# A conditioned transformer and Mamba kernel: loads in the order of use, and where the modulations are computed

## What is computed

```python
# layer 0, as one sequence sees it (t = 256, c = 256, 16 heads of 16)
mod = silu(condition) @ Wada + bada                   # 6 x 256
sh_a, sc_a, gt_a, sh_m, sc_m, gt_m = split(mod)
xm = layernorm(x, g1, be1) * (1 + sc_a) + sh_a
x = x + gt_a * (softmax(causal(q @ k.T / 4)) @ v @ Wproj + bproj)   # q, k, v = xm @ Wqkv
xm = layernorm(x, g2, be2) * (1 + sc_m) + sh_m
x = x + gt_m * (gelu(xm @ W1 + b1) @ W2 + b2)
# layer 1: (shift, scale, gate) = c @ adaln_w + adaln_b, twice
h = norm(x) * (1 + scale) + shift
x = x + gate * (ssm(h, fwd) + flip(ssm(flip(h), bwd)))
# ssm: xs, z = h @ in_w; dt, B, C = xs @ xproj_w; a scan over 256 steps,
# 512 channels x 64 states, with A = -exp(A_log); then (y + D * xs) * silu(z) @ out_w
x = x + gate * ((silu(h @ w1) * (h @ w2)) @ w3)
```

## Time and profile before

| what | value |
|---|---|
| median of 3 runs | 3541.03 us (3540.88 to 3542.23) |
| the profiled execution, its own time | 3532.22 us |
| its span in the trace | 3530.3 us |
| busy: PE, DVE, ACT, POOL | 87%, 81%, 87%, 83% |
| first projection starts | 55.99 us |
| prologue ends, first scan starts | 228.45 us |

### The profile page before, as it was taken

One profiled execution on the slowest core, in us unless ns is written; L12 is line 12 of the kernel. 1 busy time (PEld: TensorE's weight loads), 2 busy tenths in 40 slices (PEclk: granted clock), 3 DMA queues, 4 the chain that ended last, 5 costly groups with the idle time before them and its releaser, 6 DMA issues.

```text
span 3530.3 us, 70435 instructions
## 1 busy us (share of the span) xinstructions
PE 3064.4 (87%) x21944; PEld 2666.9 (76%) x21944; DVE 2872.2 (81%) x3122; ACT 3086.7 (87%) x6820; POOL 2941.0 (83%) x1551
## 2 busy tenths in 40 slices
PE   6878898898988999888998889889898899988776
PEld 4567787787877877787787778778777788877765
DVE  1249998799888998789888898889988898889885
ACT  1269999999899998899998999999998999999995
POOL 0049988899888998889888898889988899899995
PEclk9589999999999999999999999999999999999999
DMA  5011111111111111111111111111111111111211
GB/s 167 0 30 45 46 42 40 48 50 45 39 48 40 52 43 40 47 47 46 43 41 46 47 46 40 48 40 51 45 41 46 45 46 44 42 43 43 54 47 27
DMA packets 170750, 162.54 MB, mean 46 GB/s; under 512 B 25834, under 2 KB 165098, under 8 KB 170356
## 3 DMA queue, kind: packets, MB, share of 16 engines
q1 hardware_dynamic: 170356, 157.69, 16.3%
HBM read 154.44 MB, written 3.18 MB: 45 GB/s over the span
## 4 chain that ended last, share of the span: by engine, by line
PE 31%; POOL 23%; issue 20%; ACT 16%; DVE 7%; SPq 1%; POOLq 0%; DMA 0%; ACTq 0%; DVEq 0%
POOL hst L395 18%; PE ps L1175 8%; PE ps L1191 7%; ACT dA L574 7%; POOL uBT L404 6%; PE ps L944 5%; ACT uBT L560 4%; DVE hst L864 3%; PE ps L953 2%; PE ps L1013 2%; PE ps L1064 1%; PE ps L991 1%; PE ps L1000 1%; PE ps L1074 1%; SPq L301 1%
## 5 line engine op out<-in xcount | busy, mean ns | idle before, releaser
L395 POOL TENSOR_TENSOR hst<-hst,C_sb 128x1024 f32<-128x1024 f32 x1024 | 2427.1, 2385 | 324.4 <-DVE hst L864 317.5
L864 DVE TENSOR_TENSOR_SCAN hst<-dA,ps 128x512 f32<-128x512 f32 x2048 | 2383.8, 1203 | 258.7 <-ACT dA L574 135.8
L574 ACT ACTIVATE dA<-dt,A 128x255 f32<-128x255 f32 x4096 | 1779.6, 500 | 102.1 <-DVE hst L864 96.8
L1175 PE MATMUL ps<-ident,uBT 128*128 128x128 f32 x8192 | 1275.3, 280 | 153.8 <-DVE hst L864 116.5
L1191 PE MATMUL ps<-ident,hst 128*128 128x128 f32 x8192 | 1273.2, 279 | 141.8 <-POOL hst L395 139.3
L1175 PEld LDWEIGHTS ps<-ident,uBT 128*128 128x128 f32 x8192 | 993.1, 145 | 286.3 <-DVE hst L864 151.0
L1191 PEld LDWEIGHTS ps<-ident,hst 128*128 128x128 f32 x8192 | 971.2, 143 | 204.0 <-POOL hst L395 203.1
L560 ACT ACTIVATE uBT<-uT,BT 128x512 f32<-128x512 f32 x1536 | 1045.6, 714 | 32.6 <-PE ps L1175 31.6
L404 POOL TENSOR_TENSOR uBT<-uT,BT 128x512 f32<-128x512 f32 x512 | 551.7, 1078 | 227.0 <-ACT uT L517 220.1
L475 ACT ACTIVATE probs<-ps,nmax 128x128 f32<-128x128 f32 (+1 forms) x256 | 104.8, 418 | 73.6 <-DVE nmax L735 73.6
L1013 PE MATMUL ps<-qk 32*128 32x256 f32 (+1 forms) x512 | 163.0, 400 | 0.6 <-DVE v L711 0.6
(11 more groups left out here) (141 smaller groups left out, 2138.3 us busy)
## 6 DMA issues: line engine op xcount, KB each, us to landing
C_sb<-c_dram SPq DMA_DIRECT2D x1024, 128.0 KB, 2.9
gate_l<-gate_rows_dram SPq DMA_DIRECT2D x16, 256.0 KB, 3.9
x_att<-in_x_dram SPq DMA_DIRECT2D x8, 256.0 KB, 3.6
w<-in_L_cond_W_dram SPq DMA_DIRECT2D x2, 1024.0 KB
out_dram<-x_glu SPq DMA_DIRECT2D x8, 256.0 KB, 3.2
hst<-in_L_cond_Wada_dram SPq DMA_DIRECT2D x1, 1536.0 KB
wg<-in_L_cond_mlp_w_dram SPq DMA_DIRECT2D x3, 512.0 KB
w_xp<-_L_cond_fwd_xproj_w_dram SPq DMA_DIRECT2D x1, 1280.0 KB
```

Source lines behind the costliest of these rows:

```text
L395: pool.tensor_tensor(h, h, C_sb[:, n % FED:n % FED + 1, :].to_broadcast([P, KI, NB]), ALU.mult).then_inc(hC_ready.sem, 1)
L574: done = act.activation(dA[:, n % NT, c, lo:hi], dt[:, d, c, lo:hi], ACT.Exp, scale=A[:, d, c, n:n + 1])
L864: dve.tensor_tensor_scan(pair(hst[:, n % NR]), pair(dA[:, n % NT]), ps[:, BANK_U + (2 * n + e) % (2 * NT), :][:, way], 0.0, ALU.mult, ALU. ...
L1175: last = pe.transpose(ps[:, BANK_U + (2 * n + e) % (2 * NT), o:o + P], uBT[:, n % NF, j, c * P:(c + 1) * P], ident[:, :])
```

## The change

The loads are issued in another order, under six semaphores in place of two: `att_in` (columns, and of Wada the columns of the first norm, its shift and scale), then x, `qkv_in`, `mods_in` (gate biases, the rest of Wada, the adaln weights), `mlp_in`, `ssm_in` and `late_in`. Wqkv's queries and keys come as they are into the tile of `xsT` (`qk_raw`); DVE copies the query weights and POOL the key weights into the padded tiles. The weights of the second adaln move from the tile `qk`, which the projections now write early, to `uT`. PE computes two modulations (the shift and scale of the first norm) ahead of the first norm; the others, 12 by-channel pieces and the four rows, are pieces of a generator of which it takes one after each step of the first heads stage. DVE makes the first norm's scale and shift behind that norm's statistics (`setup_attention`), and everything else at the last step of the first heads stage (`setup_rest`). ACT computes exp(A) and the negation behind `layer0(0)`. The waits are set where each thing is used first.

```diff
@@ -231,7 +231,8 @@
-        wada1 = [flat(uBT[:, :, :, :].rearrange("p r k n -> p r (k n)"), 3 * D), flat(qk[:, :, :], 3 * D)]
+        wada1 = [flat(uBT[:, :, :, :].rearrange("p r k n -> p r (k n)"), 3 * D), flat(uT[:, :, :], 3 * D)]
+        qk_raw = flat(xsT[:, :, :], 2 * D)
         mod_rows = gT[0:B, :, :].rearrange("p a b -> p (a b)")
...
@@ -283,24 +286,28 @@
-            sp.dma_start(col_in[:, :], columns).then_inc(mods_in, 16)
+            def load(w, src, arrived):
+                sp.dma_start(w, src.rearrange("(k p) n -> p k n", p=P)).then_inc(arrived, 16)
+            sp.dma_start(col_in[:, :], columns).then_inc(att_in, 16)
+            load(wada[:, :, 0:2 * D], Wada[:, 0:2 * D], att_in)
+            sp.dma_start(x_att[:, :, :], x_tiles[:, 0:TT, :]).then_inc(x_in.sem, 16)
+            load(qk_raw, Wqkv[:, 0:2 * D], qkv_in)
+            load(wv[:, :, :], Wqkv[:, 2 * D:3 * D], qkv_in)
             sp.dma_start(gate_bias, rows[:, 0:4 * D].rearrange("a (i n) -> a i n", n=D)).then_inc(mods_in, 16)
-            sp.dma_start(wada, Wada.rearrange("(k p) n -> p k n", p=P)).then_inc(mods_in, 16)
-            sp.dma_start(wada1[0], wmamba.rearrange("(k p) n -> p k n", p=P)).then_inc(mods_in, 16)
-            sp.dma_start(wada1[1], wglu.rearrange("(k p) n -> p k n", p=P)).then_inc(mods_in, 16)
-            sp.dma_start(x_att[:, :, :], x_tiles[:, 0:TT, :]).then_inc(x_in.sem, 16)
-            sp.wait_ge(pads_zero, 2)
-            for w, c in ((wq, 0), (wk, 1)):
-                for k in range(KD):
-                    sp.dma_start(w[:, k, :, 0:HD], Wqkv[k * P:(k + 1) * P, c * D:(c + 1) * D]
-                                 .rearrange("p (h e) -> p h e", e=HD)).then_inc(weights_in, 16)
-            sp.dma_start(wv[:, :, :], Wqkv[:, 2 * D:3 * D].rearrange("(k p) n -> p k n", p=P)).then_inc(weights_in, 16)
-            loads = [(wproj, Wproj), (w1, W1), (w2, W2), (w_in[0], f_in), (w_in[1], b_in), (w_xp[0], f_xproj),
-                     (w_xp[1], b_xproj), (w_out[0], f_out), (w_out[1], b_out), (wg1, glu_w1), (wg2, glu_w2), (wg3, glu_w3)]
-            for w, src in loads:
-                sp.dma_start(w[:, :, :], src.rearrange("(k p) n -> p k n", p=P)).then_inc(weights_in, 16)
-            sp.dma_start(A[:, :, :, :].rearrange("p d k n -> p (d k n)"), A_log).then_inc(weights_in, 16)
-            sp.dma_start(bias_rows, rows[:, 4 * D:6 * D].rearrange("a (i n) -> a i n", n=D)).then_inc(weights_in, 16)
+            load(wada[:, :, 2 * D:6 * D], Wada[:, 2 * D:6 * D], mods_in)
+            load(wada1[0], wmamba, mods_in)
+            load(wada1[1], wglu, mods_in)
+            sp.dma_start(bias_rows, rows[:, 4 * D:6 * D].rearrange("a (i n) -> a i n", n=D)).then_inc(mlp_in, 16)
+            load(wproj[:, :, :], Wproj, mlp_in)
+            load(w1[:, :, :], W1, mlp_in)
+            load(w2[:, :, :], W2, mlp_in)
+            load(w_in[0][:, :, :], f_in, ssm_in)
+            load(w_xp[0][:, :, :], f_xproj, ssm_in)
+            sp.dma_start(A[:, :, :, :].rearrange("p d k n -> p (d k n)"), A_log).then_inc(ssm_in, 16)
+            for w, src in ((w_out[0], f_out), (w_in[1], b_in), (w_xp[1], b_xproj), (w_out[1], b_out),
+                           (wg1, glu_w1), (wg2, glu_w2), (wg3, glu_w3)):
+                load(w[:, :, :], src, late_in)
...
@@ -362,7 +369,11 @@
             sp.wait_ge(out_done.sem, out_done.at(NBLK - 1, 16))
 
-        N_MODS, N_WEIGHTS = 16 * 5, 16 * (5 + 12 + 2)
+        N_ATT, N_QKV, N_MODS, N_MLP, N_SSM, N_LATE = 16 * 2, 16 * 2, 16 * 4, 16 * 4, 16 * 3, 16 * 7
+        heads_at = STEPS["norm"] + STEPS["qkv"]
+        proj_at = heads_at + 2 * STEPS["heads"]
...
+            pool.wait_ge(pads_zero, 2)
+            pool.wait_ge(qkv_in, N_QKV)
+            pool.tensor_copy(wk[:, :, :, 0:HD], heads_of(1)).then_inc(wqk_ready, 1)
...
 
         @block.scalar
         def _(act):
-            act.wait_ge(mods_in, N_MODS)
+            act.wait_ge(att_in, N_ATT)
             act.activation(silu_col[:, :, :], cond_col, ACT.Silu).then_inc(silu_ready, 1)
             act.preload_act_table_set(LN_EXP)
-            act.wait_ge(weights_in, N_WEIGHTS)
-            act.activation(A[:, :, :, :], A[:, :, :, :], ACT.Exp).then_inc(A_ready, 1)
-            act.wait_ge(A_ready, 2)
-            act.wait_ge(mods_ready, 1)
             act.wait_ge(consts_ready, 7)
 
...
 
-            for _ in layer0(0):
-                pass
+            for i, _ in enumerate(layer0(0)):
+                if i == 4:
+                    act.wait_ge(att_mods, 1)
+                if i == proj_at - 1:
+                    act.wait_ge(mods_ready, 1)
+            act.wait_ge(ssm_in, N_SSM)
+            act.activation(A[:, :, :, :], A[:, :, :, :], ACT.Exp).then_inc(A_ready, 1)
+            act.wait_ge(A_ready, 1)
+            act.activation(A[:, :, :, :], A[:, :, :, :], ACT.Copy, scale=-1.0).then_inc(A_ready, 1)
+            act.wait_ge(A_ready, 2)
...
@@ -645,30 +663,47 @@
-            dve.wait_ge(mods_mm, 1)
-            dve.wait_ge(mods_in, N_MODS)
-            dve.tensor_copy(mod_rows, ps[0:B, 1:3, :].rearrange("p a n -> p (a n)")).then_inc(rows_ready, 1)
-            first(dve.tensor_tensor(mods[:, :, :, :].rearrange("p i k b -> p (i k) b"),
-                                    ps[:, 0, 0:16 * B].rearrange("p (i b) -> p i b", b=B),
-                                    mod_bias.rearrange("p i k -> p (i k)").unsqueeze(2).to_broadcast([P, 16, B]), ALU.add))
-
-            for s in range(4):
+            def modulations(lo, hi):
...
+            def scales(s):
...
-                    first(dve.tensor_tensor(mod_shift[:, s], mod_shift[:, s], mods[:, 2 * s], ALU.add))
-                else:
-                    first(dve.tensor_scalar(mod_scale[:, s], mods[:, 2 * s + 1], 1.0, None, ALU.add))
-                    first(dve.tensor_copy(mod_shift[:, s], mods[:, 2 * s]))
-            dve.wait_ge(A_ready, 1)
-            dve.tensor_scalar(A[:, :, :, :], A[:, :, :, :], -1.0, None, ALU.mult).then_inc(A_ready, 1)
-            dve.wait_ge(consts_ready, 7)
-            dve.wait_ge(weights_in, N_WEIGHTS)
-            for d in range(2):
-                for c in range(KI):
-                    dve.tensor_scalar(skip_diag[:, d, c, :], ident[:, :], D_col[:, d, c:c + 1], None, ALU.mult).then_inc(mods_ready, 1)
+                    return dve.tensor_tensor(mod_shift[:, s], mod_shift[:, s], mods[:, 2 * s], ALU.add)
+                first(dve.tensor_scalar(mod_scale[:, s], mods[:, 2 * s + 1], 1.0, None, ALU.add))
+                return dve.tensor_copy(mod_shift[:, s], mods[:, 2 * s])
+            def setup_attention():
+                dve.wait_ge(att_in, N_ATT)
+                dve.wait_ge(att_mm, 1)
+                modulations(0, 2)
+                scales(LN_ATT).then_inc(att_mods, 1)
+                dve.wait_ge(pads_zero, 2)
+                dve.wait_ge(qkv_in, N_QKV)
+                dve.tensor_copy(wq[:, :, :, 0:HD], heads_of(0)).then_inc(wqk_ready, 1)
+            def setup_rest():
+                dve.wait_ge(mods_mm, 1)
+                dve.tensor_copy(mod_rows, ps[0:B, 1:3, :].rearrange("p a n -> p (a n)")).then_inc(rows_ready, 1)
+                modulations(2, 8)
+                first(scales(LN_MLP))
+                first(scales(LN_SSM))
+                scales(LN_GLU).then_inc(mods_ready, 1)
+                dve.wait_ge(consts_ready, 7)
+                for d in range(2):
+                    for c in range(KI):
+                        dve.tensor_scalar(skip_diag[:, d, c, :], ident[:, :], D_col[:, d, c:c + 1], None, ALU.mult).then_inc(skip_ready, 1)
...
-            for _ in layer0(0):
-                pass
+            for i, _ in enumerate(layer0(0)):
+                if i == 0:
+                    setup_attention()
+                if i == heads_at + STEPS["heads"] - 1:
+                    setup_rest()
...
-            pe.wait_ge(silu_ready, 1)
-            pe.wait_ge(mods_in, N_MODS)
-            pe.wait_ge(consts_ready, 7)
             of_kind = [(wada, 1, 0), (wada, 1, 1), (wada, 1, 3), (wada, 1, 4),
                        (wada1[0], 0, 0), (wada1[0], 0, 1), (wada1[1], 0, 0), (wada1[1], 0, 1)]
             conds = (cond_col, silu_col)
-            for i, (w, cn, col) in enumerate(of_kind):
+            def modulation(i, m):
+                w, cn, col = of_kind[i]
+                o = (i * KD + m) * B
+                for k in range(KD):
+                    last = pe.matmul(ps[:, 0, o:o + B], w[:, k, col * D + m * P:col * D + (m + 1) * P], conds[cn][:, k, :],
+                                     start=(k == 0), stop=(k == KD - 1))
+                return last
+            def other_modulations():
+                pe.wait_ge(mods_in, N_MODS)
+                for i in range(2, 8):
+                    for m in range(KD):
+                        modulation(i, m)
+                        yield
+                for i, (w, cn, col) in enumerate(((wada, 1, 2), (wada, 1, 5), (wada1[0], 0, 2), (wada1[1], 0, 2))):
```

(42 more changed lines are left out.)

10 lines of the change are left out of this document (9 added, 1 removed).

## The result

The changed kernel took 3514.22 us, the median of 4 runs (3508.43 to 3518.37), against 3540.95 for the kernel before: 26.7 us less, a ratio of 0.9921 with an interval from 0.9905 to 0.9937. The forecast was 3515.6, 25.4 us less, in a range from 3500 to 3526. In a later series on one chip the same two kernels took 3518.3 (6 runs) and 3539.2 us (18 runs), 21 us apart. Executions in the slow state (in all three, of 3732, 8432 and 15633 us) are left out of every median here.

A forecast was written before the change was run, and what follows sets the result against it. Prologue loading was taken as the bound the change could move, each microsecond there counting at the end. 43.8 - 15.8 - 2.6 = 25.4 us less, so 3541.03 - 25.4 = 3515.6 us, range 3500 to 3526.

The forecast's parts named there:

- part 1: Prologue: reordered loads let the first norm and projections start early, first projection at 12.2 us, 43.8 us earlier.
- part 2: First heads stage: 36 modulation matmuls on PE, only partly covered by its idle time, add 15.8 us.
- part 3: Between the two heads stages: DVE's setup delays the ninth group's maximum by 2.6 us, at most 4.5.
- part 4: ACT's exp(A) and negation behind the prologue's last norm, and later load waits: 0 us; ACT's operations 1.3 us without cover.
- part 5: PE's clock rise at projections, MLP and SSM varies, 1.5 to 1.7 us each; taken as 0.
- the carry-over: Whole kernel: the runs' median lies 8.8 us above the profiled execution, assumed to hold after the change too.
- (a): Heads: filled heads keep PE's clock up, so modulations add about 0; 41.2 us gained, 3499.8 us; chance 0.12.
- (b): Nothing covers the additions: PE 21.3 us, DVE 4.5, copies or fetch 1, clock 3.4; 3527.4 us; chance 0.12.
- (c): Prologue: loads land out of issue order, x at worst at 39 us; 3548 to 3555 us, slower; chance 0.04.
- (d): Prologue: PE's queue reaches a wait early and holds the first projections, a few microseconds of 43.8; no separate chance.

The follow-up runs named there:

- The doubled set: Changed kernel with each of the 36 modulation matmuls among the heads issued twice; 3529.59 us (7 runs).
- the block: Changed kernel with the 36 other modulation matmuls in one block between the projections and the first heads stage; 3512.75 us (4 runs).

## Why the prediction was right

**Earlier start (part 1).** Right, 44.2 for 43.8. In order of issue and by bytes: silu at 5.10 (forecast 5.5), x at 5.8 (6.4), the raw weights at 8.2 (8.0), all at 41 (39). The copies were priced at no more than 1.08 us and took 0.62 and 0.42; with 1.6 us to spare they cost nothing.

**Modulations among heads (part 2).** Right, 15.1 for 15.8. The doubled set cost 20.3 for 21.2 us of matmuls, the block 17.8 over heads alone, and single ones in the gaps nothing: that PE is the bound in heads and offers half a microsecond a group is shown from three sides. The clock fell 3.7 us into heads, at 27.8 us, where about 4 us was put.

**DVE between the stages (part 3).** Right, 2.3 for 2.6; taking the diagonals out gave 1.56 of their 1.65 us back.

**Edits at nothing (part 4).** Right for the later waits: the stretch from the maximum to the first residual is the same to 0.1 us. Wrong for ACT's work on A, a term put at nothing that cost 1.3 us. The prediction set the two operations against the 8.25 us of idle time ahead of the silu, and these two are covered. It missed the table load that stands between the norm and that idle time in the kernel before, and that now runs behind the wait. Its price without cover, 1.3 us, was for the two operations and agrees by chance. No run puts exp(A) elsewhere, so that it is this move that holds the load back is read from the traces and not tested. In all, then, the change is worth 44.2 - 15.1 - 2.3 - 1.3 = 25.4 us, the very number of the forecast, because errors of 0.4, 0.7 and 0.3 us in the three terms happened to make up for the missed one.

**The clock (part 5) and the carry-over.** Here a term was mis-sized. I took 0 with a worst case of 3.4 us; between the two profiled executions it was 10.0 us ahead of the scan. The step behind it was that only the rise at the start of a dense stretch could vary, at the projections, the MLP and the SSM. The later rises came to 2.3 us, inside the worst case. The rows after show a second way, worth 7.8 us: a fall at the end of PE's 2.5 us wait for the gelu, which runs half of a product at half speed (3.3 us), and one in its 3.2 us wait for the silu, which slows the next three products (4.4). And the sum was made on an execution in which neither had happened: "3506.8 would be its counterpart" was wrong for the profiled one, 3518.4, and the first scan came at 213.1 us and not near 203. The median came out because carrying the 8.8 us over put such losses back in. The second profile of the kernel before, 3541.8 us, has 5.3 us of them ahead of the scan, in the MLP, and 4.3 behind it. That part was luck in the choice of row, not insight. The fall in the wait for the silu wasn't seen in the kernel before. Of the nine profiled executions with the longer wait it came in two, both of the changed kernel as it is, so whether it belongs to the change or to chance isn't shown.

**The rivals.** (a) That the filled heads hold the clock failed for the modulations and held for another filling: these two kinds of matmul didn't keep it up even with PE busy without a gap, while with two 256-column products with a full weight in each group it stayed up through all eight groups of the first stage. The Trainium skill's "TensorE: Matmul & The Clock Gate", section "What's actually happening", puts the clock down to how busy PE has been; the block of modulations, busy 18 of 18 us while the clock fell, disagrees if busy time is meant. (b) didn't happen as a whole; its items cost 15.1 us for PE, 2.3 for DVE and 0 for copies, and its clock item was the one that was too small. (c) was kept out by the order of the landings, and costs a little less than was worked out: 3544.6 measured, 3548 to 3555 forecast. (d) nothing held the first projection.

## What to carry to other kernels

Cut two profiles at the same few events and compare stretch by stretch: a change of 25 us in 3540 could be read to a microsecond here although runs of one kernel differ by 10, and the stretches that weren't touched show what is chance. Work that is moved out of a wait into a busy stage isn't free because it is split up; here it was free only in pieces that fit the idle time of the engine that it lands on, which is worth another 14 us. When an operation is moved into idle time, look at what else stands around that idle time: two short operations on ACT fitted, and a table load that had been hidden there came out behind the wait. And where a matrix engine runs a long stage of small products at half clock, dense products without use can pay for themselves, but try it: one version gained 22 us over the same kernel without them, and a close relative of it was 9 us slower than that kernel.

## What the hardware showed that was not expected

- PE busy 4.00 of 4.00 us with 128-column weights and 8 moving columns saw its clock fall from 1.00 to 0.54 and then 0.50; heads plus modulations were busy 32.00 of 32 us at 0.50. With two more f32 products of 256 columns in each group of 3.0 us it was at 1.00 from 24 to 40 us.
- Whether the clock falls in the same wait of 2.5 us differs from one execution to the next: the MLP's second product took 3.72 us a half in one, and 6.76 and 3.72 us in another of the same kernel. Executions of one kernel on one core mostly lay 10 to 16 us apart, between 3 and 40 us at the ends.
- A table load on ACT took 1.28 us; with two other operations ahead of it, it ran after the wait for the silu's input (180.00 us) and no longer before it (191.53 us in the kernel before, the input being there at 201.06).
- Transfers on one queue landed by bytes in the order of issue to within 0.6 us over the first 1.6 MB, and 512 elements cost POOL 0.62 and DVE 0.42 us to copy into slots of twice their width.
